# Half-length sums on the vector engine for two of eight weighted products, and a new order of pieces on four engines

## The chip, the cores and the metric

The kernel runs on one core of a Trainium2 chip. The metric is the device time of one execution in microseconds (us). The core has four computing engines that run their own instruction streams and meet only at semaphores: PE (TensorE), DVE (VectorE), ACT (ScalarE) and POOL (GpSimd); SP issues most of the DMAs.

## What is computed

Thirty-two sequences of 256 tokens with 128 channels go through two layers, each an attention part and a feed-forward part. The change is in the first layer's attention, whose last steps are, for each of four circuits c:

```python
amps = jnp.sqrt(probs + 1e-12)
w = amps * jnp.cos(coh_phase)
weighted = jnp.einsum('bsij,bsjd->bsid', w.astype(jnp.complex64), vq)
co = weighted * coh
amp = jnp.clip(jnp.abs(co), ERR_MIN, 1.0)
contrib = sup_w[c] * corrected
final = contrib if final is None else final + contrib
measured = jnp.real(final).reshape(B, S, E)
return measured @ W_out.T + b_out
```

`i` and `j` run over 8 heads and `d` over 16 channels of a head, so a token's `weighted` is, for each circuit, a sum over 8 heads j of products with 128 elements each. The second layer's attention has 16 heads over 256 tokens, and its feed-forward part sends chosen tokens to 8 experts.

## The kernel before, in words

A sequence lies in two tiles of 128 tokens (t = 0, 1) on 128 partitions. Its work up to the experts is cut into five stages, written as Python generators, one for each engine that takes part: **A** (normalise, project, turn the states: `vector_a`, `gpsimd_a`, ...), **C** (patterns, amplitudes, weighted products and their output projection), **B** (first feed-forward part, and the normalisation behind it), **E** (second attention: scores, exponents, turning and the value products) and **D** (output projection of the second attention, last normalisation, routing). Each `yield` ends a piece. A loop over b (`sequences`) works on five sequences at once: A of b, C of b-1, B of b-2, E and D of b-3. In which order an engine takes the pieces is written out by hand in a string for each engine, `POOL_ORDER`, `ACT_ORDER`, `PE_ORDER` and `DVE_ORDER`: "C1A1" means one piece of C, then one of A. Engines issue in order, so a piece that waits holds back all that stands behind it. After the loop the experts follow, with no part of these strings in them.

The steps which the change and the prediction touch, in the order in which a loop round reaches them:

- On DVE: L517 and L518 reduce the squares for A; L528 writes the new state, L538 to L541 the first turning step, L545, L548, L550, L552 the second and again the third one (`vector_a`). L580 to L586 are C's patterns, L596 to L608 its softmax. L833/L834 take the maxima of a pair of score heads (E, eight times a round). L812/L813 are the gating products of B, L819 adds its result, L792 and L800 take the statistics behind it.
- The weighted products (L652, `weighted`): eight for a sequence, k = 4t + c, each 128x1024, into one of three buffers `wprod`. DVE makes k = 0, 1, 2, 4, 5, 6; POOL makes k = 3 and 7 (`ON_POOL`). Product k waits until PE has summed product k-3 (`a_wsum`). PE sums the eight heads of a product by eight matmuls with the identity, accumulating in PSUM (L774). ACT takes the magnitude of four sums at a time (L742), DVE clips it (L660, L661), PE projects (L782, one after the other for both tiles), and DVE adds the residual (L635), the last DVE step of a round.
- On POOL: L481 to L486 are the scale of a normalisation (`norm_scale`; used by A, twice by B, by D), L680 the cross terms of the turning (two instructions), L685 the sum for its control factor, L652 the two products, L701 a bias for the residual, L896 the gates.
- D's chain: PE turns the attention's output (L1095), DVE divides (L843, L844), PE turns again (L1099, L1100), ACT copies (L974), PE projects (L1104), DVE adds (L853) and takes statistics (L859, L867), POOL scales (L481 to L486), ACT normalises (L490), PE turns (L1109), ACT copies (L981), PE routes (L1114), DVE and ACT make the gates (L872 to L880, L986).
- B's second normalisation: POOL scales, ACT normalises (L490 with `xn_e`), and E of the next round begins with PE's turning of it (L1022).

Of the kernel before, what the change touches and what calls it, by code (L numbers as in the profile page):

```python
# [9 lines left out]
ALU = mybir.AluOpType  # L10
# [6 lines left out]
NH, HD = 8, 16  # L17
# [21 lines left out]


DVE_A_STEPS = 15
DVE_C_STEPS = 19
DVE_B_STEPS = 12
DVE_D_STEPS = 8

# [4 lines left out]
ACT_START = "A3S1A3"  # L50
PE_START = "S2A1S1A1S1"
DVE_START = "S1A2S5A2S2A2S1A2S1A2S1A2S1A2S1A2S1A1S1"
POOL_ORDER = "A1C2B1A4C1B1A2C1D1C1D1"
ACT_ORDER = "E7A1E1A1E3A1E5B1E4B1E3C1A1E2B1E3C1E3B1A1E2C1E6A1E1B1D1C1D1C1D2"
PE_ORDER = "E4A1E1A1E6B1E4B1E7B1E2B1E3C1E1C1E1C1E1C1D1C1D1C1D1C2D2C2"
DVE_ORDER = "C1A1C1A1C1B1C1E1B1E1C2A1E1C1A1C1E1C2E1C2A1C1E1A1C1B1C1B1A1C1E1A1C2B1C1B1C1E1B1A1C1A1C2B2A2C2A1D2C2D3C1A2C2D2A1D2A1C1"


def build(nc, A, out):
# [8 lines left out]
    with ctx:  # L68
# [8 lines left out]
        def S(name):  # L77
            if name not in sems:
                sems[name] = ctx.enter_context(nc.semaphore(name))
            return sems[name]  # L80
# [69 lines left out]
        NWP = 3  # L150
# [34 lines left out]
        wprod = first("wprod", [P, NWP, 1024])  # L185
# [22 lines left out]
        start = carver(first.at)  # L208
# [284 lines left out]
        link_a, count_a = chain("dve_a", DVE_A_STEPS)  # L493
        link_c, count_c = chain("dve_c", DVE_C_STEPS)
        link_b, count_b = chain("dve_b", DVE_B_STEPS)
# [73 lines left out]
        def vector_c(v, b):  # L569
            count_c[0] = 0  # L570
            L = lambda ins: link_c(v, b, ins)
# [41 lines left out]
            for t in range(T):  # L613
                for c in range(NC):
                    k = t * NC + c
                    if k and k not in ON_POOL:
                        yield

                    if k not in ON_POOL:
                        if k >= NWP:  # L620
                            v.wait_ge(S("a_wsum"), 8 * b + k - NWP + 1)
                        weighted(v, t, c).then_inc(S("a_wprod"), 1)
                    if k == 6:
                        yield
                        yield from vector_clip(v, b, 0)
# [9 lines left out]
            v.tensor_tensor(x1[:, :, :], x0[:, :, :], pa[:, :, 0:128], ALU.add).then_inc(S("x1_ready"), 1)  # L635
            assert count_c[0] == DVE_C_STEPS, count_c[0]
            yield
# [8 lines left out]
            return heads(a).unsqueeze(1).broadcast_to([P, NH, NH, HD])  # L646

        ON_POOL = (3, 7)

        def weighted(eng, t, c):  # L650
            k = t * NC + c
            return eng.tensor_tensor(wprod[:, k % NWP, :].rearrange("p (j i d) -> p j i d", j=NH, d=HD),  # L652
                                     amps[:, c, t, :, :].rearrange("p i j -> p j i").unsqueeze(3).broadcast_to([P, NH, NH, HD]),
                                     v_enc[:, t, :].rearrange("p (j d) -> p j d", d=HD).unsqueeze(2).broadcast_to([P, NH, NH, HD]),
                                     ALU.mult)
# [103 lines left out]
        def tensor_c(pe, b):  # L759
            for t in range(T):  # L760
                for c in range(NC):
                    k = t * NC + c
                    if k:
                        yield
                    elif not (isinstance(b, int) and b == B - 1):
                        pe.wait_ge(S("a_qkvb"), b + 2)
                    if k == 0 and not (isinstance(b, int) and b == 0):
                        pe.wait_ge(S("x2_ready"), b)
                    if k in ON_POOL:
                        pe.wait_ge(S("a_wpool"), 2 * b + k // NC + 1)  # L770
                    else:
                        pe.wait_ge(S("a_wprod"), 6 * b + k - k // NC + 1)
                    for j in range(NH):
                        mm = pe.matmul(pa[:, t, c * P:c * P + P], wprod[:, k % NWP, j * 128:j * 128 + 128], ident[:, :],  # L774
                                       start=(j == 0), stop=(j == NH - 1))
                    mm.then_inc(S("a_wsum"), 1)
            for t in range(T):
                yield
                pe.wait_ge(S("a_clip"), 2 * b + t + 1)
                o = pa[:, t, 0:128]  # L780
                for c in range(NC):
                    mm = pe.matmul(o, clipped[:, t, c * P:c * P + P], w_out_t[:, c, :], start=(c == 0), stop=(c == NC - 1))  # L782
            mm.then_inc(S("a_y"), 1)
            yield
# [703 lines left out]
        def _(g):  # L1488
            setup_gpsimd(g)
            together(g, {"A": gpsimd_a}, {"A": 0, "S": 0}, POOL_START)  # L1490
            stages = dict(A=gpsimd_a, C=gpsimd_c, B=gpsimd_b, D=gpsimd_d)
            sequences(g, POOL_ORDER, **stages)
            gpsimd_numbers(g)
            together(g, stages, LAST_BUT_ONE, POOL_ORDER)
            for k in range(NM):
                gpsimd_gather(g, k)
            together(g, stages, LAST, POOL_ORDER)
            for k in range(NM, NG * NM):
# [3 lines left out]
        def _(act):  # L1502
# [3 lines left out]
            stages = dict(A=scalar_a, C=scalar_c, B=scalar_b, E=scalar_e, D=scalar_d)  # L1506
            sequences(act, ACT_ORDER, **stages)
            together(act, stages, LAST_BUT_ONE, ACT_ORDER)
# [61 lines left out]
```

## Time and profile before

| | us |
|---|---|
| median of 3 runs | 2515.89 |
| lowest, highest | 2506.96, 2516.02 |
| the profiled execution's own time | 2518.26 |
| its span, first to last instruction | 2516.5 |
| PE busy | 1978.0 (79%) |
| DVE busy | 1928.1 (77%) |
| ACT busy | 1262.5 (50%) |
| POOL busy | 1360.5 (54%) |

The span is the time between the first and the last instruction; the execution's own time has 1.8 us around it. The loop over the sequences takes the first 1970 us or so, the experts the rest. A busy share is an average over both.

### The profile page before, as it was taken

To read this page: it belongs to the slowest core of one execution; us is meant where nothing else is said; L and a number is where in the kernel's file an instruction comes from. 1 tells how busy PE (TensorE), PEld (TensorE's weight loads), DVE (VectorE), ACT (ScalarE), POOL (GpSimd) and SP (SyncE) were. 2 spreads that over 40 slices of the span, in tenths; PEclk is the share of its full clock that TensorE was granted. 3 is DMA by queue.
4 is the path that set the end of the run, shared out by engine and by line. 5 is a ranking of instruction groups with operands and counts; after the bars stand their busy time and mean duration, and the time that the engine had idled before them with its cause. 6 is when DMAs were issued, how large, how long until landed. Compare 5 with 4: busy or idle time off the path is not lost. (4 is left out here: it accounts for less than half of the span.)

```text
span 2516.5 us, 43496 instructions
## 1 busy us (share of the span) xinstructions
PE 1978.0 (79%) x14556; PEld 1538.8 (61%) x14556; DVE 1928.1 (77%) x3471; ACT 1262.5 (50%) x2982; POOL 1360.5 (54%) x1106
## 2 busy tenths in 40 slices
PE   1478888888888888888888888888888836758699
PEld 0466666666666666666666666666666624647477
DVE  8989899999988999989989888999998511512223
ACT  2256555555555555655655556666655413303132
POOL 5656666666666666666666666666663253142200
PEclk9889889999989999989998899999898857879799
DMA  3000000000000000000000000000000011020110
GB/s 93 5 5 10 9 8 8 8 8 8 10 8 10 8 10 8 10 8 8 8 8 8 8 8 8 8 8 8 8 6 7 5 38 36 11 67 14 54 34 26
DMA packets 64577, 39.56 MB, mean 16 GB/s; under 512 B 9350, under 2 KB 60431, under 8 KB 64528
## 3 DMA queue, kind: packets, MB, share of 16 engines
q1 hardware_dynamic: 60386, 30.51, 4.3%
q0 software_dynamic: 4096, 8.40, 1.2%
q8 instruction: 31, 0.51, 0.1%
q14 instruction: 18, 0.15, 0.0%
q10 hardware_dynamic: 46, 0.00, 0.0%
HBM read 26.31 MB, written 12.58 MB: 15 GB/s over the span
## 5 line engine op out<-in xcount | busy, mean ns | idle before, releaser
L774 PE MATMUL pa<-ident,arena 128*128 128x128 f32 x4096 | 530.7, 286 | 56.8 <-DVE arena L652 52.5
L774 PEld LDWEIGHTS pa<-ident,arena 128*128 128x128 f32 x4096 | 503.0, 201 | 74.0 <-DVE arena L652 35.3
L1059 PE MATMUL pb<-ident,arena 128*128 128x128 f32 x1536 | 290.6, 302 | 157.0 <-ACT arena L954 142.0
L1059 PEld LDWEIGHTS pb<-ident,arena 128*128 128x128 f32 x1536 | 187.6, 153 | 275.4 <-issue 187.6
L954 ACT ACTIVATE arena<-pb 128x384 f32<-128x384 f32 x512 | 252.5, 493 | 188.2 <-PE pb L1059 152.1
L680 POOL TENSOR_TENSOR arena<-state,c_cross 128x448 f32<-128x448 f32 x128 | 203.3, 1608 | 206.1 <-DVE state L541 201.3
L672 POOL TENSOR_TENSOR arena<-arena,neg_half 128x32 f32<-128x32 f32 x64 | 264.9, 4158 | 83.7 <-DVE arena L518 83.7
L652 POOL TENSOR_TENSOR arena<-arena 128x1024 f32<-128x1024 f32 x64 | 150.3, 2348 | 195.2 <-PE pa L774 195.2
L947 ACT ACTIVATE arena<-pd,arena 128x256 f32<-128x256 f32 x512 | 245.1, 479 | 0.0
L652 DVE TENSOR_TENSOR arena<-arena 128x1024 f32<-128x1024 f32 x192 | 235.9, 1254 | 2.6 <-PE pa L774 2.2
L946 ACT ACTIVATE arena<-pd,arena 128x128 f32<-128x128 f32 x512 | 188.8, 369 | 67.1 <-DVE arena L834 65.0
L1338 ACT ACTIVATE arena<-pd,b 128x512 f32<-128x512 f32 x128 | 87.4, 687 | 253.8 <-PE pd L1354 218.8
L481 POOL TENSOR_TENSOR arena<-arena,eps_t 128x2 f32<-128x2 f32 x128 | 105.2, 822 | 195.5 <-DVE arena L513 107.8
L1243 POOL DMA_INDIRECT arena<-xn_scratch,arena x128 | 121.5, 949 | 161.5 <-PE pd L1256 69.5
L484 POOL TENSOR_TENSOR arena<-arena,neg_half 128x2 f32<-128x2 f32 x128 | 170.4, 1331 | 10.0
L834 DVE TENSOR_REDUCE arena<-pd 128x2 f32<-128x512 f32 x256 | 173.6, 678 | 0.0
L833 DVE TENSOR_REDUCE arena<-pd 128x2 f32<-128x256 f32 x256 | 105.9, 414 | 82.5 <-PE pd L1050 51.9
L1310 DVE TENSOR_TENSOR arena<-pa,arena 64x512 f32<-64x512 f32 x64 | 44.1, 689 | 162.4 <-PE pa L1364 120.2
L1050 PE MATMUL pd<-arena 32*128 32x256 f32 x1024 | 160.4, 391 | 0.0
L582 DVE TENSOR_REDUCE arena<-arena 128x128 f32<-128x2048 f32 x64 | 145.9, 2280 | 0.1
L1364 PEld LDWEIGHTS pa<-w,arena 128*128 128x128 f32 x1024 | 121.8, 194 | 36.3 <-issue 36.3
L1364 PE MATMUL pa<-w,arena 128*128 128x128 f32 x1024 | 124.0, 278 | 21.5 <-issue 21.4
(250 smaller groups left out, 4403.0 us busy)
## 6 DMA issues: line engine op xcount, KB each, us to landing
x_land<-in_L_attn_query SPq DMA_DIRECT2D x32, 128.0 KB, 2.1
arena<-in_L_attn_query SPq DMA_DIRECT2D x32, 128.0 KB, 2.1
x_scratch<-x SPq DMA_DIRECT2D x32, 128.0 KB, 1.8
xn_scratch<-xn_d SPq DMA_DIRECT2D x32, 128.0 KB, 1.8
arena<-x_scratch SPq DMA_DIRECT2D x16, 256.0 KB
out_x<-arena SPq DMA_DIRECT2D x16, 256.0 KB
w<-in_L_ffn_W SPq DMA_DIRECT2D x1, 2048.0 KB
arena<-xn_scratch,arena POOLq DMA_INDIRECT x128
```

Source lines behind the costliest of these rows:

```text
L484: g.tensor_tensor(rstd[:, :], var[:, :], neg_half[:, 0:2], ALU.pow).then_inc(S(steps), 1)
L652: return eng.tensor_tensor(wprod[:, k % NWP, :].rearrange("p (j i d) -> p j i d", j=NH, d=HD), amps[:, c, t, :, :].rearrange("p i j -> p j ...
L672: g.tensor_tensor(of_tile(rnorm)[:, :, c], of_tile(ssq)[:, :, c], of_tile(neg_half)[:, :, c], ALU.pow).then_inc(S("a_rnorm"), 1)
L680: ins = g.tensor_tensor(gate_r[:, c, :, :], st[:, 1 - c, :, HD:E], c_cross[:, l, 0:GW].unsqueeze(1).broadcast_to([P, 4, GW]), ALU.mult)
L774: mm = pe.matmul(pa[:, t, c * P:c * P + P], wprod[:, k % NWP, j * 128:j * 128 + 128], ident[:, :], start=(j == 0), stop=(j == NH - 1))
L834: v.tensor_reduce(n_max[:, 1, 2 * n:2 * n + 2], pd[:, s, 128:384], AX, ALU.min).then_inc(S("b_m"), 1)
L946: act.activation(p[:, 0:128], bank[:, 0:128], ACT.Exp, bias=n_max[:, 0, s:s + 1], scale=-1.0)
L947: act.activation(p[:, 128:384], bank[:, 128:384], ACT.Exp, bias=n_max[:, 1, s:s + 1], scale=-1.0)\
L954: act.activation(p_t[:, s % 8, :], pb[:, 0:384], ACT.Copy).then_inc(S("b_pt"), 1)
L1050: mm = pe.matmul(o[:, 128:384], q_m[rows_of, r, P:2 * P], k_t[rows_of, :], start=False, stop=True, skip_group_check=True)
L1059: mm = pe.transpose(pb[:, j * P:j * P + P], p_raw[:, s % 3, j * P:j * P + P], ident[:, :])
L1364: mm = pe.matmul(o, h_act[:, e % 2, f, m * P:m * P + P], w2[:, e, f, :], start=(f == 0), stop=(f == NF - 1))
```

## The change

Products k = 2 and 6 (`HALVED`) get a second DVE instruction, which adds the upper 512 elements of the product to the lower 512 in place; PE then sums them with four matmuls instead of eight. The two extra chained steps raise `DVE_C_STEPS` by two and give stage C two more pieces on DVE. The four order strings are written anew. Everything behind line 622 moves down by five to seven lines, so that L652 is now L658, L550 is unmoved, L660 is L666, L774 is L781, L853 is L860, L680 is L686 and L685 is L691. The new addition is L625.

```diff
-DVE_C_STEPS = 19
+DVE_C_STEPS = 21
...
-POOL_ORDER = "A1C2B1A4C1B1A2C1D1C1D1"
+POOL_ORDER = "A1C2B1A4C1A1C1A1D1B1C1D1"
...
                     if k not in ON_POOL:
                         if k >= NWP:
                             v.wait_ge(S("a_wsum"), 8 * b + k - NWP + 1)
-                        weighted(v, t, c).then_inc(S("a_wprod"), 1)
+                        if k in HALVED:
+                            yield from L(weighted(v, t, c))
+                            w = wprod[:, k % NWP, :]
+                            v.tensor_tensor(w[:, 0:512], w[:, 0:512], w[:, 512:1024], ALU.add).then_inc(S("a_wprod"), 1)
+                        else:
+                            weighted(v, t, c).then_inc(S("a_wprod"), 1)
...
         ON_POOL = (3, 7)
+        HALVED = (2, 6)
...
-                    for j in range(NH):
+                    n = NH // 2 if k in HALVED else NH
+                    for j in range(n):
                         mm = pe.matmul(pa[:, t, c * P:c * P + P], wprod[:, k % NWP, j * 128:j * 128 + 128], ident[:, :],
-                                       start=(j == 0), stop=(j == NH - 1))
+                                       start=(j == 0), stop=(j == n - 1))
```

The other three strings change in the same way as POOL's. Two places of the new order matter below.

POOL, the second part of a loop round, before: product 3, the scale of B's second normalisation (the rows that wait for `dve_b` and `b_scale`), then the third turning step's cross terms.

```order
L652 TENSOR_TENSOR arena<-arena 128x1024 [waits a_wsum]
L887 REGISTER_ALU
L481 TENSOR_TENSOR arena<-arena,eps_t 128x2 [waits dve_b]
L482 TENSOR_TENSOR arena<-arena,minus_one 128x2
L483 ISA
L484 TENSOR_TENSOR arena<-arena,neg_half 128x2 [waits b_scale]
L485 REGISTER_ALU
L486 TENSOR_TENSOR arena<-arena 128x2 [waits b_scale]
L680 TENSOR_TENSOR arena<-state,c_cross 128x448 [waits a_state]
L680 TENSOR_TENSOR arena<-state,c_cross 128x448
L685 TENSOR_TENSOR arena<-arena 128x448 [waits a_m]
```

And after the change, from product 3 on; the rows that wait for `dve_d` are the scale of D's normalisation.

```order
L658 TENSOR_TENSOR arena<-arena 128x1024 [waits a_wsum]
L686 TENSOR_TENSOR arena<-state,c_cross 128x448 [waits a_state]
L686 TENSOR_TENSOR arena<-state,c_cross 128x448
L703 REGISTER_ALU [waits a_amps]
L658 TENSOR_TENSOR arena<-arena 128x1024 [waits a_wsum]
L691 TENSOR_TENSOR arena<-arena 128x448 [waits a_m]
L899 ISA
L481 TENSOR_TENSOR arena<-arena,eps_t 128x2 [waits dve_d]
L482 TENSOR_TENSOR arena<-arena,minus_one 128x2
```

B's scale has moved behind D's, and product 7 ahead of the control sum L685.

DVE, the stretch of the weighted products, before: from products 1 and 2 (one row) to product 4.

```order
L652 TENSOR_TENSOR arena<-arena 128x1024 x2
L792 BN_STATS arena<-arena 128x6 [waits x2_ready]
L792 BN_STATS arena<-arena 128x6
L794 REGISTER_ALU
L796 MEMSET spare 128x1 [waits dve_b]
L800 BN_AGGR arena<-arena 128x2 x2
L280 REGISTER_ALU
L550 TENSOR_TENSOR arena<-arena 128x896 [waits a_ctrl,dve_a]
L280 REGISTER_ALU
L552 TENSOR_TENSOR state<-state,arena 128x8x112 [waits dve_a]
L621 ISA
L652 TENSOR_TENSOR arena<-arena 128x1024 [waits a_wsum]
```

After the change, the rows that follow products 1 and 2; L840 and L841 are the eighth pair of score maxima, the last two rows products 4 and 5, and the next computing row behind them is L552.

```order
L840 TENSOR_REDUCE arena<-pd 128x2 [waits b_s]
L841 TENSOR_REDUCE arena<-pd 128x2
L799 BN_STATS arena<-arena 128x6 [waits x2_ready]
L799 BN_STATS arena<-arena 128x6
L280 REGISTER_ALU
L625 TENSOR_TENSOR arena<-arena 128x512 [waits dve_c]
L280 REGISTER_ALU
L550 TENSOR_TENSOR arena<-arena 128x896 [waits a_ctrl,dve_a]
L621 ISA
L658 TENSOR_TENSOR arena<-arena 128x1024 [waits a_wsum]
L621 REGISTER_ALU
L658 TENSOR_TENSOR arena<-arena 128x1024 [waits a_wsum]
```

L548, which stood between product 0 and product 1, has moved ahead of product 0. The pair of maxima, the new addition and products 4 and 5 now stand ahead of L552, which releases POOL's cross terms for the third turning step. Behind L552 come L545, product 6, L850 and L851 (L843 and L844 before), the second addition, and D's L860 (L853 before). On PE, the turning and the projection of D (L1099, L1100 and L1104 before) now follow each other with no sum between them; before, the sum of product 5 stood there. On ACT, the normalisation that uses B's second scale (L490 with `xn_e`) now stands behind the copy L981 and ahead of the exponents L986 of the same round.

## Rows read from the trace of the kernel before

**Rows 1.** The page's costliest groups: busy, mean ns of one, idle before; two on DVE.
```profile
L834 DVE TENSOR_REDUCE arena<-pd 128x2 f32<-128x512 f32 x256 | 173.6, 678 | 0.0
L833 DVE TENSOR_REDUCE arena<-pd 128x2 f32<-128x256 f32 x256 | 105.9, 414 | 82.5 <-PE pd L1050 51.9
```

**Rows 2.** Busy time in windows cut at L635: two rounds, and 16 rounds together.
```profile
core 0: us, PE busy (x) PEld busy (x) DVE busy (x) ACT busy (x) POOL busy (x), PEclk, DMA share, GB/s
...
1000.31:1059.23 58.92, 48.44 (x396) 38.30 (x394) 55.18 (x97) 35.84 (x88) 38.34 (x30) 0.96 0.03 9
1059.23:1122.59 63.36, 54.49 (x395) 42.81 (x394) 55.14 (x98) 36.17 (x88) 38.62 (x31) 0.85 0.03 8
...
sum 968.44, PE 804.98 PEld 631.36 DVE 883.45 ACT 574.25 POOL 621.74; mean PE 50.31 PEld 39.46 DVE 55.22 ACT 35.89 POOL 38.86
```

**Rows 3.** Timeline of DVE, second part of the round from 1000.31: start, us, line, shapes, idle before.
```profile
1033.83 1.21 DVE L652 TENSOR_TENSOR arena<-arena 128x1024 f32<-128x1024 f32 x1
...
1035.97 2.35 DVE L652 TENSOR_TENSOR arena<-arena 128x1024 f32<-128x1024 f32 x2
...
1038.92 2.46 DVE L550 TENSOR_TENSOR arena<-arena 128x896 f32<-128x896 f32 x1
1041.41 1.10 DVE L552 TENSOR_TENSOR state<-state,arena 128x896 f32<-128x896 f32 x1
...
1050.69 0.42 DVE L853 TENSOR_TENSOR x<-arena,pd 128x256 f32<-128x256 f32 x1 [0.60 <-PE pd L1104]
...
1053.53 1.09 DVE L550 TENSOR_TENSOR arena<-arena 128x896 f32<-128x896 f32 x1
1056.10 0.43 DVE L660 TENSOR_SCALAR arena<-arena 128x512 f32<-128x512 f32 x1 [1.48 <-ACT arena L742]
```

**Rows 4.** Timeline of POOL in the same round.
```profile
1028.75 2.35 POOL L680 TENSOR_TENSOR arena<-state,c_cross 128x448 f32<-128x448 f32 x2 [6.37 <-DVE state L541]
...
1038.41 2.02 POOL L652 TENSOR_TENSOR arena<-arena 128x1024 f32<-128x1024 f32 x1 [5.77 <-PE pa L774]
...
1043.66 4.07 POOL L680 TENSOR_TENSOR arena<-state,c_cross 128x448 f32<-128x448 f32 x2
...
1049.76 2.20 POOL L652 TENSOR_TENSOR arena<-arena 128x1024 f32<-128x1024 f32 x1
1052.00 0.20 POOL L481 TENSOR_TENSOR arena<-arena,eps_t 128x2 f32<-128x2 f32 x1
```

**Rows 5.** Timeline of ACT in the same round: D's normalisation and the second magnitude.
```profile
1054.71 0.88 ACT L490 ACTIVATE xn_d<-x,arena 128x128 f32<-128x128 f32 x2 [5.57 <-POOL arena L486]
1055.49 0.57 ACT L742 ACTIVATE arena<-pa 128x512 f32<-128x512 f32 x1
```

**Rows 6.** Timeline of PE in the same round: first sum, last two sums, D's turning, projection.
```profile
1035.10 3.23 PE L774 MATMUL pa<-ident,arena 128*128 128x128 f32 x16 [1.00 <-DVE arena L652]
...
1050.30 3.77 PE L774 MATMUL pa<-ident,arena 128*128 128x128 f32 x32
1055.64 0.44 PE L1109 MATMUL pd<-ident,xn_d 128*128 128x128 f32 x2 [1.57 <-ACT xn_d L490]
...
1057.02 2.03 PE L782 MATMUL pa<-w_out_t,arena 128*128 128x128 f32 x16
```

**Rows 7.** The projection on PE and the residual on DVE at the end of the round from 1059.23.
```profile
1118.69 3.76 PE L782 MATMUL pa<-w_out_t,arena 128*128 128x128 f32 x16
...
1122.59 0.42 DVE L635 TENSOR_TENSOR arena<-arena,pa 128x256 f32<-128x256 f32 x1 [1.60 <-PE pa L782]
```

**Rows 8.** Groups by line and shape over the whole execution: busy, mean ns, idle before.
```profile
L652 POOL TENSOR_TENSOR arena<-arena 128x1024 f32<-128x1024 f32 x64 | 150.3, 2348 | 195.2 <-PE pa L774 195.2
L517 DVE TENSOR_REDUCE arena<-arena 128x48 f32<-128x768 f32 x32 | 30.3, 948 | 18.2 <-ACT arena L716 18.2
L528 DVE TENSOR_TENSOR state<-arena 128x512 f32<-128x512 f32 x32 | 21.8, 682 | 0.8 <-POOL arena L672 0.8
L539 DVE TENSOR_TENSOR arena<-arena,c_diag 128x448 f32<-128x448 f32 x32 | 19.7, 615 | 0.0
```

More of the change, by code:

```diff
@@ L52 @@
 DVE_START = "S1A2S5A2S2A2S1A2S1A2S1A2S1A2S1A2S1A1S1"
-POOL_ORDER = "A1C2B1A4C1B1A2C1D1C1D1"
-ACT_ORDER = "E7A1E1A1E3A1E5B1E4B1E3C1A1E2B1E3C1E3B1A1E2C1E6A1E1B1D1C1D1C1D2"
-PE_ORDER = "E4A1E1A1E6B1E4B1E7B1E2B1E3C1E1C1E1C1E1C1D1C1D1C1D1C2D2C2"
-DVE_ORDER = "C1A1C1A1C1B1C1E1B1E1C2A1E1C1A1C1E1C2E1C2A1C1E1A1C1B1C1B1A1C1E1A1C2B1C1B1C1E1B1A1C1A1C2B2A2C2A1D2C2D3C1A2C2D2A1D2A1C1"
+POOL_ORDER = "A1C2B1A4C1A1C1A1D1B1C1D1"
+ACT_ORDER = "E7A1E1A1E4A1E4B1E4B1E3A1C1E1B1E2C1E3A1B1E3C1E8A1C1D2C1D1B1D1"
+PE_ORDER = "E4A1E1A1E8B1E2B1E7B1E2B1E2C1E1C1E1C1E2C1D1C1D2C3D2C2"
+DVE_ORDER = "C1A1C1A1C1B1C1E1C1E1C1B1C1A1E1A1C1E1C3E1C1A1C1A1C1A1C1E1B1C1A1C1B1C1E1C1B1C1A1B1A1B1C3E1B1C1A1C2A2C1D2C1B1D1C1D2C1A2C2D2A1D1A1D1C1"
 def build(nc, A, out):
```

## The prediction

> **What bounds the kernel now.** Read the windows first, cut at L635, the last DVE step of a round [rows 2]. Sixteen rounds take 968.4 us, 60.5 each; DVE is busy 55.2 of them, PE 50.3, POOL 38.9. A quick round takes 58.92 us at a granted TensorE clock of 0.96, a slow one 63.36 at 0.85, with the same DVE work: the loop has two nearly full engines, and about 5 us a round in which DVE waits. About 29 such rounds make the time; the experts, the last 550 us, aren't touched.
>
> Then the timelines of one quick round say which waits end last. I count from the start of product 0 at 1033.83, "+" from there. The first part (58.92 less 25.40) takes 33.52 us and DVE hardly waits in it. In the second part DVE waits for the second magnitude, 1.48 us before L660 at +22.3 [rows 3]. ACT held that magnitude back (+21.7) because it stands behind D's normalisation, at +20.9, whose scale POOL gave [rows 5]. POOL began that scale at +18.2, in the moment in which product 7 left it; D's statistics were in at that time too [rows 4]. Behind it come PE's turning at +21.8, the projection L782 at +23.2 and L635 at +25.4 [rows 6]. So the second part is paced by **POOL's queue**: the cross terms start at +9.8 behind B's scale, the control sum and product 7 follow, and D's scale ends it. PE's last two sums are over at +20.2 and 1.57 us of PE idle follows [rows 6]: they aren't last.
>
> **The change, term by term, for one round.**
>
> 1. PE loses half of two sums. The last two full sums, 32 records, took 3.77 us, 0.118 each, so a half sum (8 records) is 0.94 us and two are 1.9 us [rows 6]. It lies ahead of PE's 1.57 us of idle, so it only makes that idle longer: worth 0 on the path here. If PE ended last, it would be worth all 1.9.
>
> 2. DVE gains two additions of 128x512 with both inputs in SBUF. L539 with 448 elements takes 0.615 us, L528 with 512 takes 0.682 [rows 8]; neighbours overlap by some 0.08, so 0.60 each, 1.2 us a round. That is less than DVE's 5 us of waiting, but they stand where things queue behind them (term 4).
>
> 3. First part. The reduction L517 now stands behind the second L581 and a BN step. Its waits, 18.2 us in 32 [rows 8], 0.57 a round, go. L548 moves from the second part to the first (+1.0), a pair of maxima the other way (0.414 + 0.678 less overlap, 0.93 [rows 1]), and the second pattern reduction's neighbours change places at no cost. I give the part -0.3 us, between -0.6 and +0.4: the far end is a control or cross term that POOL holds when L548, now earlier, wants it.
>
> 4. Second part. Behind products 0, 1, 2 (to +3.4) come the maxima (0.93, to +4.3), two statistics (0.4), the first addition, L550, products 4 and 5 (2.3), L552 (1.1). The two forms of L550 give the price of standing beside POOL: 1.09 us alone, 2.46 beside POOL's product [rows 3]; it ended about 1 us behind the end of the product. POOL's product 3 ran from +4.6 to +6.6 here [rows 4], and can start at +3.4 if PE's first sum isn't at the low clock (that sum took 3.23 us in place of 1.9 [rows 6]). So the addition ends at +6.0 to +7.2, L550 at +7.0 to +8.2, and L552 at **+10.4 to +11.6**, where it ended at +8.7 before [rows 3].
>
> The Trainium skill (SBUF — State Buffer, Who interferes with whom) says that a DVE instruction with two SBUF inputs and a GpSimd instruction that reads SBUF exclude each other for the whole instruction. By it an addition could be held by a whole POOL product, where L550's stretch shows 1.4 us; this trace agrees with the exclusion in kind, and the sum keeps to the 1.4.
>
> 5. POOL's cross terms can't start before L552. Before, they started at +9.8, because B's scale stood ahead of them; that scale has gone behind D's, but the start moves to +10.4 to +11.6 all the same. From there to D's scale the same POOL work follows as before, which took 8.3 us (+9.8 to +18.2) [rows 4]: cross terms 4.07 beside DVE's work against 2.35 alone, L685, product 7 in 2.20. Beside it now stand L545, product 6, one more addition and L666 on DVE, so I don't expect the 8.3 to shrink; ends 7.6 and 9.0. D's scale then starts at +18.0 to +20.6, where it was +18.2; a quick round gives **+18.9**, and the late product 3, seen in about half of the rounds, adds 1.2. I take +0.8 in the mean after a discount, since the low clock that makes product 3 late also makes other things late in the round of before.
>
> 6. D's input. PE must wait for L851, behind product 6 on DVE, then for ACT's copy, with no sum between: some 2 us of PE idle. L552's end at +10.4, L545 (1.1), half of the cross terms (1.2), product 6 (1.1), L850 and L851 (0.6) and 1.4 for PE's turning, the copy and the projection put L860 at about +15.8, where L853 stood at +16.9 [rows 3], so D's statistics are in at about +18.5. They are earlier than needed: worth 0. Cover: POOL's queue; if that were quicker than I say, this gain would show.
>
> 7. Round's end. B's scale now runs behind D's, 2.7 us or so, ACT's normalisation 0.88 behind it, and the exponents L986 behind that; DVE's gate sum L884 and the residual L640 wait for them. By the same steps they are ready 0.1 to 0.4 us behind PE's projection. I take +0.2, ends 0 and +0.6.
>
> Sum: -0.3 + 0.8 + 0.2 = **+0.7 us a round**, 29 rounds: +20 us. Ends: -0.6 - 0.2 + 0 = -0.8, and +0.4 + 2.4 + 0.6 = +3.4. Against the profiled execution's own 2518.3 that is 2538.6; the median of the runs is 2.4 lower, so I say **2537 us**. A measurement of this kernel can tell about 0.5%, 12.6 us, from no change, which is 0.43 us a round.
>
> **The rivals.**
>
> *Faster: PE ends last after all.* In rounds like that from 1059.23 the clock is 0.85 and PE is busy 54.5 of 63.4 us [rows 2]; DVE waits for PE in both parts. There 1.9 us of matmuls, more at the low clock, plus the 0.6 of L517 are on the path, and more slack for the projection's start helps. If the two parts gain what PE loses wherever the round is longer than the quick one (60.5 less 58.9, 1.6 us in the mean) and POOL's chain slips by only 0.4, a round gains 1.2 us: 2516 - 35 = **2481 us**. It decides from the point where D's scale starts no later than at +18.2. For it: 5 us of DVE waiting. Against: PE's idle of 1.57 us ahead of D's turning. Chance 0.30.
>
> *No change.* Terms 3 and 5 cancel: L552 at +9.8, reached if the addition and L550 never stand beside POOL. Then -0.3 + 0.1 + 0.1, **2513 us**. Chance 0.23.
>
> *Slower by the clock.* The projection took 2.03 us in the quick round and 3.76 in the slow one [rows 6, 7], and L635 waited for it. PE went idle for 1.57 us before it [rows 6]. With 1.9 us less of sums and the same chain, that idle grows to 3 us or more, and PE may come to the projection at the low level (1.2 GHz in place of 2.4) each round. That adds up to 1.7 us where it doesn't happen yet, about half of the rounds, so 0.9 on top of my 0.7: 2516 + 46 = **2562 us**. The Trainium skill (TensorE: Matmul & The Clock Gate, What's actually happening) says that activity releases the throttle and idleness sets it; by that the saved matmuls are paid back, and the slow rounds' clock agrees. Chance 0.15, within "slower".
>
> *My forecast,* POOL's chain slips by about 0.8: chance 0.32.
>
> **How the numbers follow.** Faster 0.30, same 0.23, slower 0.32 + 0.15 = 0.47. The forecast is the likeliest, 2537; its own range is 2515 to 2560. The range over all cases runs from just beyond the faster case, 2475, to beyond the clock's, 2580; the outer ends of the sum (2493 and 2615) are reached only if all terms fall one way.
>
> **What would show it.** Right: in quick rounds L552's end of the second step at +10.4 or later, POOL's cross terms directly behind it, D's scale at +18.9 or later, the round at 60 us or more with DVE busy at about 56.5; L517 without a wait; PE busy 1.9 us less. Wrong: D's scale before +18.2, or the slow rounds (63.4) shorter by more than 1.5 us while the quick ones keep their 58.9. If L635 (now L640) waits for ACT's exponents and not for PE, term 7 was too small. If the projection takes 3.8 us in most rounds, the clock rival is at work.

## The result, and the profile after

The changed kernel takes 2520.89 us (median of 20 runs, 2514.41 to 2528.25); the kernel before, run beside it, 2515.7 (20 runs). The ratio of the means is **1.0031, 95% interval 1.0016 to 1.0047**: some 8 us slower (5.2 between the medians), where 21 were forecast. The interval leaves out 1, but the difference is below the 0.5% that the prediction took as what can be told from no change. The profiled execution's own time is 2526.06, its span 2523.7; the last L640 starts at 1974.89, where the last L635 started at 1968.30, so 6.6 us of it is in the loop.

The page, instructions and busy time:

```profile
span 2523.7 us, 42593 instructions
...
PE 1945.2 (77%) x14044; PEld 1475.9 (58%) x14044; DVE 1944.9 (77%) x3535; ACT 1274.7 (51%) x2982; POOL 1252.5 (50%) x1106
```

PE gave up 33 us of its 1978.0, DVE gained 17 on its 1928.1, POOL lost 108. Next the windows from the second round's L635 to the thirtieth's, 28 rounds in one row. Before:

```profile
214.84:1910.24 1695.40, 1411.20 (x11034) 1108.95 (x11032) 1544.35 (x2688) 1005.15 (x2464) 1087.30 (x840) 0.93 0.03 9
```

After, cut at L640 (columns as in [rows 2]), then a quick round and a slow one behind it:

```profile
214.45:1914.29 1699.84, 1377.14 (x10586) 1049.34 (x10584) 1556.91 (x2745) 1016.83 (x2464) 986.88 (x840) 0.92 0.03 9
...
1124.22:1183.26 59.04, 47.29 (x380) 35.89 (x378) 55.46 (x99) 36.32 (x89) 35.03 (x29) 0.96 0.03 9
1183.26:1245.69 62.43, 51.37 (x378) 38.97 (x378) 55.81 (x100) 36.43 (x88) 35.46 (x31) 0.89 0.03 8
```

A round takes 1699.84 / 28 = 60.71 us, before 60.55: **+0.16**, where +0.7 was forecast. DVE works 55.60 a round, 0.45 more, though the additions alone are 68.4 us in 32 sequences, 2.1 a round:

```profile
L658 DVE TENSOR_TENSOR arena<-arena 128x1024 f32<-128x1024 f32 x192 | 255.4, 1369 | 6.2 <-PE pa L781 5.7 <-ACT arena L743 0.4
L545 DVE TENSOR_TENSOR arena<-state,c_diag 128x896 f32<-128x896 f32 x64 | 71.9, 1124 | 1.1
L550 DVE TENSOR_TENSOR arena<-arena 128x896 f32<-128x896 f32 x64 | 70.0, 1093 | 1.1
L625 DVE TENSOR_TENSOR arena<-arena 128x512 f32<-128x512 f32 x64 | 68.4, 1068 | 0.1
L666 DVE TENSOR_SCALAR arena<-arena 128x512 f32<-128x512 f32 x64 | 52.6, 821 | 45.9 <-ACT arena L748 45.9
L517 DVE TENSOR_REDUCE arena<-arena 128x48 f32<-128x768 f32 x32 | 30.3, 946 | 5.0 <-ACT arena L722 4.6
L640 DVE TENSOR_TENSOR arena<-arena,pa 128x256 f32<-128x256 f32 x32 | 13.3, 417 | 24.7 <-PE pa L789 24.7
```

In the kernel before, L550 and L545 took longer:

```profile
L550 DVE TENSOR_TENSOR arena<-arena 128x896 f32<-128x896 f32 x64 | 106.5, 1664 | 1.1
L545 DVE TENSOR_TENSOR arena<-state,c_diag 128x896 f32<-128x896 f32 x64 | 99.7, 1559 | 0.1
```

These two take 64.3 us less: as the rows below show, L550 now stands behind POOL's product and L545 begins just ahead of the cross terms. L658 (+19.5 over L652 of before) and L666 (+6.1 over L660) take some of it again, because one product and one clipping now stand there.

The second part of the quick round after, on DVE. Product 0 starts at 1157.96, which is "+0".

```profile
1157.96 3.49 DVE L658 TENSOR_TENSOR arena<-arena 128x1024 f32<-128x1024 f32 x3
...
1162.68 1.24 DVE L625 TENSOR_TENSOR arena<-arena 128x512 f32<-128x512 f32 x1
1163.85 1.08 DVE L550 TENSOR_TENSOR arena<-arena 128x896 f32<-128x896 f32 x1
...
1167.12 1.08 DVE L552 TENSOR_TENSOR state<-state,arena 128x896 f32<-128x896 f32 x1
1168.23 1.09 DVE L545 TENSOR_TENSOR arena<-state,c_diag 128x896 f32<-128x896 f32 x1
1169.24 2.16 DVE L658 TENSOR_TENSOR arena<-arena 128x1024 f32<-128x1024 f32 x1
...
1172.05 0.89 DVE L625 TENSOR_TENSOR arena<-arena 128x512 f32<-128x512 f32 x1
...
1174.04 0.42 DVE L860 TENSOR_TENSOR x<-arena,pd 128x256 f32<-128x256 f32 x1 [0.93 <-PE pd L1111]
...
1179.95 0.87 DVE L666 TENSOR_SCALAR arena<-arena 128x512 f32<-128x512 f32 x1 [1.48 <-ACT arena L748]
```

And on POOL:

```profile
1161.36 2.01 POOL L658 TENSOR_TENSOR arena<-arena 128x1024 f32<-128x1024 f32 x1 [6.54 <-PE pa L781]
1168.28 4.11 POOL L686 TENSOR_TENSOR arena<-state,c_cross 128x448 f32<-128x448 f32 x2 [4.90 <-DVE state L552]
1172.35 2.46 POOL L658 TENSOR_TENSOR arena<-arena 128x1024 f32<-128x1024 f32 x1
1174.77 1.32 POOL L691 TENSOR_TENSOR arena<-arena 128x448 f32<-128x448 f32 x1
1176.05 0.19 POOL L481 TENSOR_TENSOR arena<-arena,eps_t 128x2 f32<-128x2 f32 x1
```

L552 ends at +10.24, the cross terms start at +10.32 directly behind it, L860 starts at +16.08, D's scale at **+18.09**, the second L666 at +21.99. Before, these last two were at +18.2 and +22.3 in the round of [rows 3, 4]; over 28 rounds, 18.03 and 22.05. PE in the same stretch:

```profile
1159.23 2.05 PE L781 MATMUL pa<-ident,arena 128*128 128x128 f32 x16 [0.64 <-DVE arena L658]
...
1180.87 2.03 PE L789 MATMUL pa<-w_out_t,arena 128*128 128x128 f32 x16
```

PE's first sum takes 2.05 us and not the 3.23 of [rows 6]. So it is in all 28 rounds after (in 12 of 28 before): product 3 starts on POOL at +3.40 each time, where before it started at +4.1 to +4.6 in 16 of 28 rounds.

### The profile page after: what moved, and what is told of

Read it like the earlier page. It is cut to its first block and busy times, and to the rows that moved or that the text cites. A ratio compares the mean times of both kernels' runs of the same rounds, so it can differ in the third digit from the quotient of the medians.

```text
span 2523.7 us, 42593 instructions
## 1 busy us (share of the span) xinstructions
PE 1945.2 (77%) x14044; PEld 1475.9 (58%) x14044; DVE 1944.9 (77%) x3535; ACT 1274.7 (51%) x2982; POOL 1252.5 (50%) x1106
## 5 line engine op out<-in xcount | busy, mean ns | idle before, releaser
L781 PE MATMUL pa<-ident,arena 128*128 128x128 f32 x3584 | 443.9, 279 | 45.8 <-DVE arena L658 40.8
L781 PEld LDWEIGHTS pa<-ident,arena 128*128 128x128 f32 x3584 | 419.3, 194 | 63.0 <-issue 30.7
L1066 PE MATMUL pb<-ident,arena 128*128 128x128 f32 x1536 | 298.6, 309 | 155.3 <-ACT arena L961 142.9
L686 POOL TENSOR_TENSOR arena<-state,c_cross 128x448 f32<-128x448 f32 x128 | 205.6, 1625 | 321.9 <-DVE state L541 169.3
L658 POOL TENSOR_TENSOR arena<-arena 128x1024 f32<-128x1024 f32 x64 | 142.8, 2232 | 239.9 <-PE pa L781 239.9
L658 DVE TENSOR_TENSOR arena<-arena 128x1024 f32<-128x1024 f32 x192 | 255.4, 1369 | 6.2 <-PE pa L781 5.7
L481 POOL TENSOR_TENSOR arena<-arena,eps_t 128x2 f32<-128x2 f32 x128 | 80.4, 628 | 221.5 <-DVE arena L513 92.0
L840 DVE TENSOR_REDUCE arena<-pd 128x2 f32<-128x256 f32 x256 | 106.8, 417 | 90.9 <-PE pd L1057 63.2
L841 DVE TENSOR_REDUCE arena<-pd 128x2 f32<-128x512 f32 x256 | 174.2, 680 | 0.0
L484 POOL TENSOR_TENSOR arena<-arena,neg_half 128x2 f32<-128x2 f32 x128 | 146.0, 1141 | 10.0
```

Source lines behind the costliest of these rows:

```text
L484: g.tensor_tensor(rstd[:, :], var[:, :], neg_half[:, 0:2], ALU.pow).then_inc(S(steps), 1)
L686: ins = g.tensor_tensor(gate_r[:, c, :, :], st[:, 1 - c, :, HD:E], c_cross[:, l, 0:GW].unsqueeze(1).broadcast_to([P, 4, GW]), ALU.mult)
L841: v.tensor_reduce(n_max[:, 1, 2 * n:2 * n + 2], pd[:, s, 128:384], AX, ALU.min).then_inc(S("b_m"), 1)
L1066: mm = pe.transpose(pb[:, j * P:j * P + P], p_raw[:, s % 3, j * P:j * P + P], ident[:, :])
```

## The experiments

They ran in three sets on three other chips, each beside the kernel before, which took 2390, 2384 and 2387 us there, some 130 us less than above; each ratio is to the kernel before on the same chip. For the changed kernel, run again with the second set, the difference lies behind the loop. Ratios below compare only among themselves. A round is 26 to 28 rounds' window divided by their number; the first part runs from L635 (L640) to product 0, the second from there to the next.

The ratios come from many executions, the other columns from one traced execution of each kernel. The changed kernel, traced twice, gives 60.71 and 60.57 us a round, so a difference of 0.1 or 0.2 us there says little.

| kernel | ratio, 95% interval | round | first part | second part | D's scale at |
|---|---|---|---|---|---|
| before | 1 | 60.55 | 34.29 | 26.26 | +18.03 |
| changed | 1.0042 [1.0022, 1.0062] | 60.57 | 34.52 | 26.05 | +18.09 |
| halves, old order | 1.0379 [1.0354, 1.0403] | 63.54 | 34.25 | 29.28 | +20.32 |
| halves, old order, second addition later | 1.0133 [1.0109, 1.0156] | 61.43 | 34.78 | 26.65 | +18.54 |
| new order, no halves | 1.0101 [1.0080, 1.0122] | 61.39 | 35.04 | 26.34 | +18.58 |
| new order, product 2 halved | 1.0118 [1.0091, 1.0146] | 61.36 | 35.22 | 26.13 | +18.53 |
| new order, product 6 halved | 1.0057 [1.0038, 1.0075] | 60.95 | 34.72 | 26.23 | +18.13 |
| changed, first projection early | 0.9989 [0.9965, 1.0013] | 60.45 | 34.99 | 25.46 | +18.09 |
| changed, both projections early | 1.0106 [1.0085, 1.0127] | 61.41 | 34.91 | 26.50 | +18.09 |
| changed, projection and magnitude early | 1.0123 [1.0101, 1.0144] | 61.41 | 36.28 | 25.13 | +18.09 |
| before, first projection early | 0.9859 [0.9832, 0.9887] | 59.35 | 34.29 | 25.06 | +17.96 |
| before, projection and magnitude early | 0.9905 [0.9881, 0.9929] | 59.75 | 34.42 | 25.34 | +18.16 |

(The row "before" is that of the first chip's trace; the row "changed" is the run with the second set.)

**The two halves of the change apart.** The changed code with the four strings of before and two pieces more on DVE; the two additions follow their products directly.

```diff
-POOL_ORDER = "A1C2B1A4C1A1C1A1D1B1C1D1"
+POOL_ORDER = "A1C2B1A4C1B1A2C1D1C1D1"
...
-DVE_ORDER = "...C3E1B1C1A1C2A2C1D2C1B1D1C1D2C1A2C2D2A1D1A1D1C1"
+DVE_ORDER = "...E1B1A1C1A1C2B2C1A2C2A1D2C3D3C1A2C2D2A1D2A1C1"
```

> The half-length sums alone, in the order of pieces of the kernel before: the additions stand on DVE between L800 and L550 and directly behind product 6. Theory Q (POOL's queue and DVE's additions decide, PE's saved matmuls only lengthen its idle): L552 ends near +9.2, below POOL's +9.6 to +9.8, and the second addition delays L660 by 0.6 us under a wait of 0.6; the round moves by 0 to +0.5 us, the ratio to the kernel before is 1.000 to 1.007. Theory P (PE's work is on the path in rounds with a low clock, and the order is what costs): the round gains 0.5 to 1.5 us, ratio 0.976 to 0.992.

And the order alone, `HALVED` gone:

```diff
-DVE_C_STEPS = 21
+DVE_C_STEPS = 19
-                        if k in HALVED:
...
+                        weighted(v, t, c).then_inc(S("a_wprod"), 1)
```

> The new order of pieces alone, all eight products summed whole, no additions. Theory Q: L552 ends about 0.6 us earlier than in the changed kernel (+9.6), POOL's chain to D's scale with it (+17.5), PE's last sum comes 1.9 us later and fills its idle; ratio to the kernel before 0.990 to 1.000, at or below the changed kernel's 1.003. Theory P: PE's full sums come back onto the path; ratio 1.008 to 1.020.

Halves alone cost 3.0 us a round (1.038), the order alone 0.84 (1.010), both 0.16: the parts are each bad without the other. The first is outside both ranges given. The second is within the range of theory P, whose reading it bears out in part: L552 ends at +10.28 and not at +9.6, because product 5 waits for PE's whole sum of product 2 (and product 6, behind L552, 0.40 us for the next). One such product 5, with product 0 at 799.33:

```profile
807.38 1.23 DVE L652 TENSOR_TENSOR arena<-arena 128x1024 f32<-128x1024 f32 x1 [0.55 <-PE pa L774]
```

The windows of the two kernels, halves first (26 rounds), then the order (27):

```profile
220.64:1872.62 1651.98, 1295.46 (x9830) 1000.30 (x9828) 1519.15 (x2548) 931.10 (x2288) 1034.53 (x780) 0.92 0.03 8
```

```profile
213.94:1871.36 1657.42, 1373.37 (x10639) 1049.81 (x10638) 1474.96 (x2595) 982.78 (x2377) 941.01 (x810) 0.93 0.03 9
```

With the halves alone PE is busy 49.83 us a round, 0.6 less than before, and the round is 3.0 longer: PE isn't what they hurt. DVE is busy 58.43 a round, 3.3 over before. Its second part in the kernel with halves alone, product 0 at 956.00:

```profile
961.08 1.82 DVE L625 TENSOR_TENSOR arena<-arena 128x512 f32<-128x512 f32 x1
...
971.35 1.51 DVE L625 TENSOR_TENSOR arena<-arena 128x512 f32<-128x512 f32 x1
972.78 2.23 DVE L666 TENSOR_SCALAR arena<-arena 128x512 f32<-128x512 f32 x1
974.94 0.41 DVE L860 TENSOR_TENSOR x<-arena,pd 128x256 f32<-128x256 f32 x1
```

And POOL beside it:

```profile
959.40 2.95 POOL L658 TENSOR_TENSOR arena<-arena 128x1024 f32<-128x1024 f32 x1 [4.59 <-PE pa L781]
...
970.20 2.11 POOL L691 TENSOR_TENSOR arena<-arena 128x448 f32<-128x448 f32 x1
972.27 2.46 POOL L658 TENSOR_TENSOR arena<-arena 128x1024 f32<-128x1024 f32 x1
976.23 0.20 POOL L481 TENSOR_TENSOR arena<-arena,eps_t 128x2 f32<-128x2 f32 x1 [1.50 <-DVE arena L874]
```

The first addition ends at 962.90, 0.55 us behind POOL's product; the second at 972.86, 0.55 behind POOL's L691. L666 then runs for as long as POOL's next product and ends at 975.01, 0.28 behind it. L860 stands behind all of them, at +18.94 without any wait of its own, and POOL, which had at most 0.28 us of gap ahead of D's scale before ([rows 4] show none), now waits 1.50 us for D's statistics. D's scale starts 2.3 us later in the mean.

**Is it that place?** The same kernel with the second addition and the first clipping moved behind D's residual and statistics.

```diff
-DVE_ORDER = "...C2B2C1A2C2A1D2C3D3C1A2C2D2A1D2A1C1"
+DVE_ORDER = "...C2B2C1A2C2A1D2C1D3C3A2C2D2A1D2A1C1"
```

> The half sums in the old order once more, with one thing moved: the second addition and the first L666 stand behind D's residual and statistics (L860 to L874) and not ahead of them. In the run with the half sums alone, the second addition took 1.51 us and the L666 behind it 2.23 us beside POOL, and L860 came at +18.9 (before: +16.6), D's scale at +20.2. If the 3.0 us that the half sums cost there is this hold-up of D's chain, L860 comes at about +16.9 here, D's scale at +18.2 to +18.6, and the round loses 0.5 to 1.2 us to the kernel before: ratio 1.006 to 1.018 in place of 1.038. If it is DVE's added work as such or PE's waits for the additions, the ratio stays over 1.025.

Measured 61.43 us a round and a ratio of 1.0133, as that expectation had it: 2.1 of the 3.0 come back. Behind L860 the same two instructions take 0.75 and 0.42 in place of 1.51 and 2.23:

```profile
1189.80 0.42 DVE L860 TENSOR_TENSOR x<-arena,pd 128x256 f32<-128x256 f32 x1 [1.61 <-PE pd L1111]
...
1190.95 0.75 DVE L625 TENSOR_TENSOR arena<-arena 128x512 f32<-128x512 f32 x1
1191.62 0.42 DVE L666 TENSOR_SCALAR arena<-arena 128x512 f32<-128x512 f32 x1
```

Of the 0.9 that stay, 0.5 are in the first part and 0.4 in the second. The first addition, which takes 1.8 to 2.5 us ahead of L550 and puts L552's end at +9.34 in the mean instead of +8.52, may be behind them; that was not tried. Of what the halves alone cost, the place of the second addition and the clipping behind it is 2.1 us in 3.0.

**Each half in the new order.** Only one product halved, one piece fewer.

```diff
-DVE_C_STEPS = 21
+DVE_C_STEPS = 20
...
-        HALVED = (2, 6)
+        HALVED = (2,)
```

> The changed kernel with the half sum for product 2 only: product 6 is summed whole and its addition is gone. The second addition stood in a time in which DVE waited 0.93 us for L860 anyway, and PE has an idle of 1.2 us behind its last sum. Reading by the chain: both the addition's cost and the saved 0.94 us are covered, the round changes by -0.2 to +0.3 us; ratio to the kernel before 1.000 to 1.008.

> The changed kernel with the half sum for product 6 only. Without the first addition (1.24 us beside POOL's product 3) L550 could end 0.6 us earlier, but DVE must wait for PE's whole sum of product 2 before product 5 (0.94 us in the run without half sums), so L552 still ends at +10.2. Reading by the chain: this is the run without half sums again in the first place, ratio 1.004 to 1.012; if the first half sum is worth nothing, the ratio is the changed kernel's.

Product 2 alone gives nothing over the bare order (61.36 to 61.39), and its ratio, 1.0118, misses the range given; product 6 alone gives 0.44; both 0.82 (60.57). The ratios say the same in smaller steps. With product 2 alone, product 6 alone and both, all on one chip, the medians are 2415.2, 2399.3 and 2395.0 us: over 31 rounds the halved product 6 is worth some 0.65 us a round beside the other one, and the halved product 2 some 0.1, within overlapping intervals. (The traced execution of product 6 alone was 8 us above its median, so the table's 60.95 is high.) The worth of product 6 isn't in PE's sum. With product 6 whole, DVE, product 0 at 1043.71:

```profile
1059.79 0.42 DVE L860 TENSOR_TENSOR x<-arena,pd 128x256 f32<-128x256 f32 x1 [1.74 <-PE pd L1111]
1060.13 1.36 DVE L666 TENSOR_SCALAR arena<-arena 128x512 f32<-128x512 f32 x1
```

and POOL:

```profile
1058.10 2.01 POOL L658 TENSOR_TENSOR arena<-arena 128x1024 f32<-128x1024 f32 x1
1060.07 1.13 POOL L691 TENSOR_TENSOR arena<-arena 128x448 f32<-128x448 f32 x1
1062.25 0.20 POOL L481 TENSOR_TENSOR arena<-arena,eps_t 128x2 f32<-128x2 f32 x1 [1.04 <-DVE arena L874]
```

L860 starts at +16.08, as after the change. But with no addition beside it, POOL's product 7 takes 2.01 us and not 2.46, L691 starts 0.45 earlier, and L666 falls beside it: 1.36 us in place of 0.72. D's statistics stand behind L666, POOL waits 1.04 for them, and D's scale starts at +18.53. In the changed kernel the second addition keeps POOL back just far enough that L666 gets in between, and POOL has no gap ahead of D's scale. Of product 2's half the trace shows another effect: with it whole, products 5 and 6 on DVE wait 0.55 and 0.40 us for PE's sums, as in the bare order; halved, there are no such waits. They cost little on the path: L552 ends at +10.28 with them and at +10.24 without.

That D's scale comes earlier is shown; how it makes the round shorter is not. The shortest second part goes from 25.93 us (product 2 alone) to 25.29 (both), but in the mean the second part is 26.1 to 26.3 in all four, and the first part, which has no weighted product in it, goes from 35.0 and 35.2 to 34.7 and 34.5. The longer first part goes with the clock: in 17 of 27 rounds of the bare order (21 with product 2 alone, 12 of 28 with product 6 alone, 10 of 28 with both) the first part is longer than 35.3 us, with L840 (L833 where no product is halved) waiting 1.4 to 1.6 us in all for PE at a low granted clock.

**Where the low clock falls.** The projection stood last on PE, and DVE waited for it (L640, 24.7 us in all). The first tile's projection can go into PE's idle time ahead of D's turning.

```diff
-PE_ORDER = "...C1E2C1D1C1D2C3D2C2"
+PE_ORDER = "...C1E2C1D1C1D2C4D2C1"
```

> The changed kernel with PE's projection of the first tile (half of L789) moved ahead of D's turning L1116, into PE's idle behind the last sum. If the end of the round is a chain from D's scale over L1116 and L1121 to the whole projection, as I read it, the second half of the projection ends 1.0 us earlier at the full clock and up to 1.9 at the low one, cut short by ACT's exponents L993 and the DVE steps behind them (L640 could start at about +24.6 without PE in a quick round, where it starts at +25.3): -0.7 to -1.3 us a round, ratio to the kernel before 0.988 to 0.995. If the clock takes it back (clock theory), or the exponents end last everywhere, it stays at 1.000 to 1.004.

The wait of L640 fell from 24.7 to 3.8 us, the second part from 26.05 to 25.46; the first part rose from 34.52 to 34.99, and nothing that can be told from none is left of it against before (0.9989, between the two ranges given). Two more kernels pull on the same end. In the first, ACT also takes the second magnitude ahead of D's normalisation and both projections go ahead of D's turning:

```diff
-ACT_ORDER = "...E8A1C1D2C1D1B1D1"
+ACT_ORDER = "...E8A1C1D1C1D2B1D1"
-PE_ORDER = "...C1E2C1D1C1D2C3D2C2"
+PE_ORDER = "...C1E2C1D1C1D2C5D2"
```

> The changed kernel with ACT's second magnitude ahead of D's normalisation and both halves of PE's projection ahead of D's turning. The magnitude then starts when PE's last sum ends (+20.3) and DVE's 1.48 us wait before the second L666 goes; the projection can end at +23, but D's turning and routing stand behind it and the exponents with them. Reading by the chain: L640 is held by the exponents at about +24.6 to +25, ratio 0.985 to 0.995; if D's routing, now behind the projection, sets the end, 0.995 to 1.005.

The second part is 26.50: the routing scores now come last (L879 waits 2.55 us for PE), and the ratio, 1.0106, is beyond both ranges: a miss. The other has the same string on ACT and only the first projection early:

> The changed kernel with ACT's second magnitude ahead of D's normalisation and the first half of PE's projection ahead of D's turning. With the projection alone moved, the second part was 25.3 to 25.9 us and DVE still waited 1.48 us for the magnitude. Reading by the chain: the magnitude starts at about +20.4, the second L666 at +21.0, and the end of the round waits for D's routing and the exponents, at +24.8 to +25.0: 0.4 us a round less, ratio to the kernel before 0.990 to 0.998. If the magnitude pushes D's normalisation back instead, 0.999 to 1.004.

One round of it, cut at product 0:

```profile
1011.25:1047.56 36.31, 31.17 (x195) 20.45 (x199) 33.19 (x62) 25.58 (x65) 21.34 (x16) 0.76 0.02 7
1047.56:1072.69 25.13, 20.59 (x188) 18.32 (x181) 22.32 (x39) 10.75 (x24) 13.97 (x14) 1.00 0.04 10
```

From the third of 27 rounds on, each takes 61.43 to 61.49 us. The second part is shorter than in any other kernel with the new order, at a clock of 1.00, and the first part is 36.31 at 0.76; the ratio, 1.0123, is beyond both ranges too. In the quick round of the changed kernel the first part has the same work; the third line is the first part of the round behind it:

```profile
1124.22:1157.96 33.74, 26.86 (x197) 17.72 (x199) 32.78 (x61) 26.03 (x66) 21.07 (x15) 0.93 0.03 8
1157.96:1183.26 25.30, 20.42 (x187) 18.17 (x179) 22.68 (x40) 10.29 (x24) 13.96 (x14) 1.00 0.04 10
...
1183.26:1219.00 35.74, 29.41 (x196) 19.17 (x200) 33.07 (x63) 26.26 (x66) 21.28 (x16) 0.86 0.02 7
```

The first part with the clock at 0.76 has 4.3 us more of PE's time than that at 0.93 for the same 195 to 197 matmuls, and is 2.6 longer. What is gained in the second part is lost in the next first part by a low clock there. The changed kernel does it too: all seven of its second parts of 25.3 us are followed by a first part of 35.5 to 35.7 (nine of nine in its second trace), and 13 of the other 20 by one of 33.7 to 33.8. It isn't a rule for every order: with the first projection early, nine of nineteen second parts of 25.3 are followed by a first part under 33.8. Why the low clock falls where it does isn't settled.

**The same move on the kernel before.** If the forecast's path was right, its projection had the same fault.

```diff
-PE_ORDER = "...C1D1C1D1C1D1C2D2C2"
+PE_ORDER = "...C1D1C1D1C1D1C3D2C1"
```

> The kernel before with the first half of PE's projection L782 moved ahead of D's turning L1109, into the 1.57 us in which PE was idle. In the changed kernel the same move made the second part of every round 25.3 to 25.9 us (26.2 in the mean before the move) and the first part 0.5 us longer. If PE's low clock only moves to another place in the round, the ratio here is 0.996 to 1.002; if the projection's place is worth its 1 to 1.9 us, 0.978 to 0.990.

0.9859: some 34 us faster than before (31 between the medians), faster than anything else here, and within the range given for the projection's place. The tail of one second part on PE, product 0 at 1017.34:

```profile
1033.28 4.04 PE L774 MATMUL pa<-ident,arena 128*128 128x128 f32 x32
1037.16 1.06 PE L782 MATMUL pa<-w_out_t,arena 128*128 128x128 f32 x8
1038.62 0.44 PE L1109 MATMUL pd<-ident,xn_d 128*128 128x128 f32 x2 [0.41 <-ACT xn_d L490]
...
1040.29 1.16 PE L782 MATMUL pa<-w_out_t,arena 128*128 128x128 f32 x8
```

Half of the projection (1.06 us) lies in what was 1.57 us of idle; L635 never waits (0.0 in all, 25.9 before) and every second part is 24.9 or 25.4. And here the first part stays at 34.29. The magnitude moved as well:

```diff
-ACT_ORDER = "...E6A1E1B1D1C1D1C1D2"
+ACT_ORDER = "...E6A1E1B1D1C2D3"
```

> The kernel before with both moves: the first half of the projection ahead of D's turning (which alone gave 0.986) and the second magnitude ahead of D's normalisation. PE's last sum ends at +20.2 and D's scale at +20.3 to +20.8, so the magnitude's 0.57 us fits between them. Chain: second L660 at +20.9 in place of +21.8 to +22.3, residual at +24.3: a further 0.3 to 0.6 us a round, ratio 0.976 to 0.984. If the low clock of PE takes it back, 0.984 to 0.990.

L660's wait falls from 1.48 to 0.39 as meant, but L872 waits 0.99 for the routing in its place, and product 3 is late in every other round: 59.75 and a ratio of 0.9905, worse than with the first move alone. A miss.

The changed kernel once more, on the chip of the second set:

> The changed kernel itself, beside the other runs, so that they can be compared with it on one chip. Ratio to the kernel before 1.001 to 1.006 if the loop's rounds are the same on every chip, as the rounds of the first four experiments suggest.

1.0042, with an interval that overlaps the first chip's.

## Why the prediction was right or wrong

**Term 1, PE's halves, worth 0 on the path.** Right for the second part's own chain: PE's busy time fell by 1.2 us a round and not by 1.9 (1411.20 to 1377.14 in 28), and D's scale hardly moved. What it left out is what the runs with one half show: in the new order the short sum of product 2 removes waits which that order makes (0.55 and 0.40 at products 5 and 6), and the first part is quicker with both halves.

**Term 2, 0.60 for each addition.** In the changed kernel they take 1.24 and 0.89, and the shortest seen is 0.75. But all of them end 0.55 us behind the POOL instruction beside which they began (here 1163.92 behind 1163.37 and 1172.94 behind 1172.39), so the 0.60 was a fair price for the work itself, and the rest is waiting. The rows of all the traces with additions agree: each addition in the loop's middle ends 0.54 to 0.56 behind a POOL instruction.

**Term 4, L552's end at +10.4 to +11.6.** Right to 0.16 us, just past its early end: +10.24 in every round. Product 3 stands at +3.40, the addition ends at +5.96, L550 at +6.97. The exclusion is of whole instructions, as those 0.55 us behind POOL's end show. That is what the Trainium skill (SBUF — State Buffer, Who interferes with whom) says; the trace agrees. The sum kept to the milder 1.4, which did no harm, because POOL's product started early.

**Term 5, +0.8 at D's scale: this is the step that failed.** The start of the cross terms was right (+10.32). "So I don't expect the 8.3 to shrink" was wrong: it took 7.77 us, 10.32 to 18.09, near the low end I gave (7.6). Of the three pieces in it, the cross terms are as long as before and product 7 is longer (2.46 for 2.20); the control sum takes 1.32 us beside a residual and a clipping, where before, beside product 6, it takes 2.11 in each of the 28 rounds:

```profile
1047.69 2.11 POOL L685 TENSOR_TENSOR arena<-arena 128x448 f32<-128x448 f32 x1
```

The second miss is the late product 3, which I had add 1.2 in half of the rounds: it never happens, in this or any other kernel of the new order, and happens in 10 to 16 of the rounds in each kernel of the old one. In the kernel before it cost little, too: D's scale started at +18.16 in the rounds with a late product 3 and at +17.85 in the others. So the term measured +0.06 (18.03 to 18.09) in place of +0.8, and the second L666 even starts 0.05 earlier. Why the new order spares PE's first sum the long form isn't settled.

**Term 3, the first part, -0.3: wrong in sign.** L517's wait mostly went (18.2 us, [rows 8], to 5.0), but the first part is 0.24 longer, which lies within the -0.6 to +0.4 for another reason than the one given. Rounds with a first part under 35.3 have it at 33.85 before and 33.88 after; but 10 of 28 are at 35.7 where 6 of 28 were at 35.9. That is a matter of where the low clock falls, which neither end of my range had in it.

**Term 6, worth 0.** Right: L860 at +16.08 (said +15.8), and POOL comes to D's scale without a gap. But its cover is thin: D's statistics are in 0.3 us ahead (the forecast had 0.4), and the run with product 6 whole shows it gone.

**Term 7, +0.2 at the round's end.** Wrong in kind: L640 waits for PE's projection (24.7 us in all, as before), never for the exponents. B's scale takes 1.38 us behind D's (1178.49 to 1179.86), and not 2.7. In the mean the whole second part is 0.08 shorter than before.

The sum: +0.24 for the first part and -0.08 for the second, in place of -0.3 + 0.8 + 0.2, so **+0.16** and not +0.7; 28 rounds are 4.4 us, the rest of the loop 2.2. (The prediction's own sum, 2538.6 less 2.4, gives 2536.2 and not 2537.)

**The rivals.** "No change" came nearest, though for another reason than its own (L552 at +9.8): L552 was as late as I said, and POOL made it good. "PE ends last" named D's scale no later than +18.2 as its point; that point was reached, but it could tell nothing, since the mean before was +18.03 already. The round wasn't quicker: the shortest second part went from 24.88 to 25.29, and more rounds have the long first part. "Slower by the clock" had its mechanism in the wrong part: the projection isn't at the low level each round (it takes 2.03 us in 7 of 28 rounds, in 8 before, and 3.76 in 3, in 7 before), but the low clock is more often in the first part. The Trainium skill (TensorE: Matmul & The Clock Gate, What's actually happening) says that idleness brings the throttle back. In the kernel with projection and magnitude early, PE is busy for 20.59 of 25.13 us of the second part, in the changed one for 20.42 of 25.30, and the first part behind it is at a low clock in both, 0.76 and 0.86. No run here varies PE's idleness alone, and with the first projection early about half of the second parts of 25.3 us have a quick first part behind them. The rows don't settle it.

**The signs.** Of those named for "right", the cross terms directly behind L552 came. D's scale at +18.9, quick rounds of 60 us (59.04) and DVE busy for 56.5 (55.6) did not, nor quite L552's end at +10.4 (10.24). Of those for "wrong", D's scale was before +18.2. The slow rounds went from 63.4 to some 62.4, less than the 1.5 named.

## What to carry to other kernels

Price an added DVE instruction by what stands on POOL at that moment and by what is queued behind it: the same addition took 0.75 us in one place; in another it took 1.51, its neighbour 1.8 more than elsewhere, and the chain behind both was late by it. Halving two of PE's sums and reordering were each a loss alone and nearly free together, so a result of one says little about both. And where an engine has idle time just ahead of its last work, look for a piece that can be moved into it before adding work elsewhere: one changed string gave 1.4%.

## What was not expected of the hardware

- A TENSOR_SCALAR of 128x512 (L666) takes 0.42 us alone and 2.23 beside POOL's product, ending 0.28 us behind it; in all traces, where it begins while a POOL product or control sum runs, it ends 0.28 or 0.29 behind that. It has one tensor input, and is held like the additions, which have two.
- Rounds repeat to 0.01 us and fall into patterns: in the changed kernel every second or third round is slow, in that with projection and magnitude early all are alike at 61.44 us. With both projections early, rounds of 62.64 and 60.23 alternate, 122.87 in two, which is twice 61.44, though the second part is 1.4 us longer there. So a local gain need not shorten the round: 25.13 us in the second part at 1.00 go with 36.31 in the first at 0.76. What sets that period isn't known.
- Two chips run the loop alike (in the changed kernel the last L640 starts at 1974.89 on one and at 1971.56 on the other), yet the part behind it, which has indirect DMAs, takes 549 us on the one and 418 on the other; which of its instructions differ was not traced further. The spans are 2523.7 and 2390.0 us. Times of this kernel from different chips can't be compared without that.
